# Output projection as side jobs of the top-16 attention, and another order of the first loads, in a graph and transformer kernel on one core

## Chip, cores and metric

The kernel runs on one core of a Trainium2 chip. The metric is the device time of one execution in microseconds.

## What is computed

Node features x (1250 x 512, float32) and 41250 edges (src, dst, sorted by dst) go through four residual layers, each on the normalised rows of x:

```
x = x + gnn0(layernorm(x))      # x@wc + mean over edges of (x@wn)[dst] + bias
x = x + ffn0(layernorm(x))      # causal attention, 8 heads, then a gated mixture of 8 experts
x = x + gnn1(layernorm(x))      # x@W_self.T + neighbour mean @ W_neigh.T, layer norm, gamma, beta
x = x + ffn1(layernorm(x))      # below
return x
```

The last layer (`_L1_ffn_ref`) is

```
x   = x + (depthwise conv over 3 rows + pos_b)
q,k,v = split(x @ qkv_w.T + qkv_b); 8 heads of 64
logits = (q * 512**-0.5) @ k.T                  # 1250 x 1250 a head
_, idx = top_k(logits, 16)                      # per row
attn   = softmax over those 16; out = attn @ v[idx]
return out @ wo_w.T + wo_b
```

## The kernel before

The rows are kept as 10 tiles of 128 (the last of 98) in the SBUF tensor `X` (`NT` = 10, `D` = 512, `KD` = 4 blocks of 128 columns, `H` = 8 heads, `HP` = 4 pairs of heads). The program is a series of stages, each a block in which the five engines run their own instruction lists and meet by semaphores; between stages all engines meet. The change touches the first stage and the last.

**First stage, `graph_in` (L94).** It builds the adjacency counts as a matrix. SP fetches the edges (`raw`, 8 DMAs, L173 and L175), then `wc`, five vectors and `v_b` broadcast to all partitions (L177 to L182), and then the list `ahead` (L185: `wn`, the three attention weights of the next layer, some vectors), all on one queue, one after the other and without waiting. ACT, on its own queue, fetches the node rows X as soon as their padding is zeroed (L396 and L398).

VectorE waits for all edge DMAs (`s_edges`), splits the indices (L234 to L237), reduces the distance of every edge from its window to a flag that says whether a slower general path is needed (`worst`, L241 to L244), and makes three keys (L246 to L249), the third for the general path alone. TensorE transposes `worst` (L333) and then the three keys, 9 transposes (L338); VectorE makes the flag (L252 to L256) and copies the keys to `ends` (L258). Then each engine loads the flag in a register and branches. With these inputs both take the Else side: for each of 323 groups of 128 edges VectorE writes two one-hot tiles (`one_hot`, L264 and L265) into one of `HOTS` = 8 buffers and TensorE multiplies them into a chunk of PSUM (L379), after opening each chunk with a matmul of zeros (L376). ACT copies finished chunks to `AT` (L465), and TensorE turns them (`flip`, L299). Between these, at written group numbers, ACT computes row means (`mean`, L403, for group 10), variances (L411, groups 22 and 36), and the normalised rows, of which TensorE makes the first layer's own projection.

**Last stage, `top_layer` (L1142).** After convolution and the first pair's projections, a loop of `TN` = 80 steps runs, one for each head and tile: n = 20*i + 10*half + t. In step n:
- SP fetched the pair's keys and queries for `half` earlier (L1236), POOL splits them in parts (`stage`).
- TensorE makes scores(n+1) in three banks of PSUM; two steps alternate between banks 0 to 2 and 3 to 5.
- VectorE (`largest`, L1682 to L1690) takes the 8 largest twice and replaces them.
- ACT takes exponentials (L1580, L1586), POOL subtracts (L1284), which leaves the 16 largest; TensorE transposes the result of step n-2 in three pieces through bank 6 (`turn`, L1405), ACT copies each piece (`keep`, L1607, L1602); for each pair of steps TensorE weighs V (`weigh`, L1420) in bank 7, ACT drains it (L1616), and POOL multiplies it by the inverse sums into `QO` (`normalise`, L1293).

Each engine's list of a step is written by hand. Bank 7 also serves side jobs, all on odd steps, in the dictionary `work_at`: the q, k and v projections of the next pair of heads (`qk` jobs of 4 float32 matmuls at steps 1 to 9 after the start of a pair, `v` jobs at 11, 13 and 15), and for the last pair, which has none to prepare, four `wo` jobs at steps 61, 63, 65 and 67 that transpose the output weights. A program counts the evictions before each step (`kept_after`, `jobs_before`, `qkv_jobs`), and these counts are the waits:

```
for b in range(KD):
    work_at[61 + 2 * b] = ("wo", b, None)
...
if (i, half) == (3, 0):
    sp.wait_ge(s_job, qkv_jobs)
    sp.dma_start(raw_wo[:, :, :], rows_of(io["L1_ffn_wo_w"])).then_inc(s_wo_in, 16)
```

TensorE issues a job's parts between the pieces of `turn` (`job`, L1448), ACT evicts it one step later (`keep_job`, L1552). `raw_wo` lies where `ct` (the convolved rows) was, `wo` where the weights `wt` were.

The output projection (`project`, L1462) of tile t is four matmuls over `QO`'s four blocks, one block a pair of heads. Tiles 0 and 1 are issued at the end of step 79, 2 and 3 after step 80, 4 and 5 after 81, and 6 to 9 after 82. POOL has added the output bias to X in steps 0 to 9 (L1313). VectorE adds each projected tile to X (L1706), and SP stores it (L1247).

Of the kernel before, what the change touches and what calls it, by code (L numbers as in the profile page):

```python
# [20 lines left out]
P = 128  # L21
# [72 lines left out]
def graph_in(nc, m, io, space, wc, own, hi, lo, ahead):  # L94
# [39 lines left out]
    with ExitStack() as ctx:  # L134
# [31 lines left out]
        @block.sync  # L166
        def _(sp):
            sp.wait_ge(s_blank, 2)
            for n, name in enumerate(("src", "dst")):
                e = io[name]  # L170
                for g in range(EG):
                    rows = min(P, full - g * P)
                    sp.dma_start(raw[0:rows, n, g, :], e[g * P * P:(g * P + rows) * P].rearrange(  # L173
                        "(t p) -> t p", p=P)).then_inc(s_edges, 16)
                sp.dma_start(raw[last_p:last_p + 1, n, last_g, 0:rest], e[full * P:NE].rearrange(  # L175
                    "(a p) -> a p", a=1)).then_inc(s_edges, 16)
            sp.dma_start(wc[:, :, :], rows_of(io["L0_gnn_wc"])).then_inc(s_wc, 16)  # L177
            for vec, small in ((m.bias0, "L0_gnn_bias"), (m.bias1, "L1_gnn_bias"), (m.gamma1, "L1_gnn_gamma"),
                               (m.beta1, "L1_gnn_beta"), (m.wo_b, "L1_ffn_wo_b")):
                sp.dma_start(vec[:, :], io[small].rearrange("(a d) -> a d", a=1).broadcast_to([P, D])  # L180
                             ).then_inc(s_small, 16)
            sp.dma_start(m.v_b[:, :], io["L1_ffn_qkv_b"][2 * D:3 * D].rearrange("(a d) -> a d", a=1)  # L182
                         .broadcast_to([P, D])).then_inc(s_small, 16)
            for dst, src in ahead[1]:
                sp.dma_start(dst, src).then_inc(ahead[0], 16)  # L185
            sp.wait_ge(s_small, 96)
            sp.wait_ge(ahead[0], 16 * len(ahead[1]))
# [27 lines left out]
        def _(dve):  # L215
# [22 lines left out]
                              ALU.subtract).then_inc(s_split, 1)  # L238
            dve.wait_ge(s_split, 3)
            drel = key[:, 3, :, :].rearrange("p g e -> p (g e)")  # L240
            dve.tensor_reduce(worst[:, 0:1], drel, AX_X, ALU.max).then_inc(s_flag, 1)  # L241
# [3 lines left out]
                                     op0=ALU.add, op1=ALU.max).then_inc(s_flag, 1)  # L245
            dve.tensor_copy(key[:, 0, :, :], part[:, 0, :, :]).then_inc(s_split, 1)  # L246
            dve.scalar_tensor_tensor(out=key[:, 1, :, :], in0=key[:, 3, :, :], scalar=float(NT), in1=part[:, 1, :, :],
                                     op0=ALU.mult, op1=ALU.add).then_inc(s_split, 1)
            dve.scalar_tensor_tensor(out=key[:, 2, :, :], in0=raw[:, 1, :, :], scalar=float(NT), in1=part[:, 1, :, :],  # L249
                                     op0=ALU.mult, op1=ALU.add).then_inc(s_split, 1)  # L250
            dve.wait_ge(s_lined, 1)
# [5 lines left out]
            dve.wait_ge(s_keyed, 1)  # L257
            dve.tensor_copy(ends[:, :, :].rearrange("p n e -> p (n e)"), ps_f[:, 0:3 * EG * P]).then_inc(s_cols, 1)  # L258
            dve.wait_ge(s_cols, 1)
# [12 lines left out]
            scattered = dve.value_load(flag_i[0:1, 0:1], min_val=0, max_val=1)  # L272
            with dve.If(scattered):
                for chunks in (range(0, 3), range(3, NC)):
                    if chunks[0]:
# [18 lines left out]
        def _(pe):  # L294
# [36 lines left out]
            pe.wait_ge(s_made, 3)  # L331
            pe.wait_ge(s_flag, 3)
            pe.transpose(ps_w[:, 0:P], worst[:, 2:3], m.identf[:, :]).then_inc(s_lined, 1)  # L333
            pe.wait_ge(s_split, 6)
            for n in range(3):
                for g in range(EG):
                    c = (n * EG + g) * P
                    mm = pe.transpose(ps_f[:, c:c + P], key[:, n, g, :], m.identf[:, :])  # L338
            mm.then_inc(s_keyed, 1)
            pe.wait_ge(s_cols, 1)  # L340
            pe.wait_ge(s_blank, 3)
# [4 lines left out]
            scattered = pe.value_load(flag_i[0:1, 0:1], min_val=0, max_val=1)  # L346
            with pe.If(scattered):
                for c in range(NC):
                    bank = ps_c[:, c % CHUNKS, :]
# [42 lines left out]
        def _(act):  # L392
            x = io["x"]
            act.wait_ge(s_zeroed, 1)
            for a in (0, 3, 6):
                act.dma_start(m.X[:, a:a + 3, :], x[a * P:(a + 3) * P, :].rearrange("(t p) d -> p t d", p=P)  # L396
                              ).then_inc(s_nodes, 16)
# [744 lines left out]
def top_layer(nc, m, io, space, raw_qk, raw_v, taps, qb, s_ahead, ahead_done, out):  # L1142
# [12 lines left out]
    for i in range(1, HP):  # L1155
        for v, job in enumerate(qk_jobs):
            work_at[2 * NT * (i - 1) + 1 + 2 * v] = ("qk", i, job)
        for v, ts in enumerate(v_groups):
            work_at[2 * NT * (i - 1) + 11 + 2 * v] = ("v", i, ts)
    for b in range(KD):  # L1160
        work_at[61 + 2 * b] = ("wo", b, None)
    evictions, jobs = len(v_groups), len(v_groups)
# [6 lines left out]
    v_kept = [len(v_groups)] + [kept_after[2 * NT * (i - 1) + 11 + 2 * (len(v_groups) - 1)] for i in range(1, HP)]  # L1169
    qkv_jobs = jobs_before[61]  # L1170

    with ExitStack() as ctx:
        s = Stage(nc, m, ctx, "tl")
        (s_zn, s_w_turned, s_w_kept, s_x_turned, s_x_kept, s_edge, s_tapped, s_mid, s_conv, s_first, s_first_kept,
         s_job, s_job_kept, s_wo_in, s_staged_k,
         s_fetched_0, s_fetched_1, s_staged, s_scored, s_max, s_negm, s_read, s_max2, s_topped, s_exp, s_rest,
         s_sum, s_inv, s_blank, s_probs, s_turned, s_kept, s_weighed, s_drained, s_normed, s_biased,
         s_projected, s_final, s_stored) = s.signals(
            "zn w_turned w_kept x_turned x_kept edge tapped mid conv first first_kept job job_kept wo_in staged_k "
            "fetched_0 fetched_1 staged scored max negm read max2 topped exp rest sum inv blank probs turned kept "  # L1180
# [6 lines left out]
        wt = space("tl_wt", 61440, [P, KD, 3 * D])  # L1187
        raw_wo = space("tl_raw_wo", 40960, [P, KD, D])
        wo = space("tl_wo", 61440, [P, KD, D])
# [36 lines left out]
        def _(sp):  # L1226
            sp.wait_ge(s_first_kept, 6)
            for i in range(HP):
                for half in range(2):
# [4 lines left out]
                    for arrived, rows in ((kl, KT[r, i % 2:i % 2 + 1, :]), (qs, QO[r, i:i + 1, :])):  # L1234
                        for to in range(2):
                            sp.dma_start(arrived[to * DH:(to + 1) * DH, half:half + 1, :].bitcast(F32), rows  # L1236
                                         ).then_inc(s_fetched[half], 16)
                    if (i, half) == (3, 0):
                        sp.wait_ge(s_job, qkv_jobs)
                        sp.dma_start(raw_wo[:, :, :], rows_of(io["L1_ffn_wo_w"])).then_inc(s_wo_in, 16)  # L1240
            for half in range(2):
                sp.wait_ge(s_fetched[half], 64 * HP)
            sp.wait_ge(s_wo_in, 16)
            for t in range(NT):
# [6 lines left out]
        def _(pool):  # L1251
# [50 lines left out]
            for n in range(TN + 4):  # L1302
# [7 lines left out]
                if 0 < hi < 2 * HP and step < 5:  # L1310
                    stage(hi, step)
                if n < NT:
                    pool.tensor_tensor(m.X[:, n, :], m.X[:, n, :], m.wo_b[:, :], ALU.add).then_inc(s_biased, 1)  # L1313
                    pool.wait_ge(s_biased, n + 1)

        @block.tensor
        def _(pe):
# [109 lines left out]
            def job(n, part):  # L1427

                kind, i, what = work_at[n]
                if part == 0:  # L1430
                    if n >= 5:
                        pe.wait_ge(s_drained, 2 * ((n - 3) // 2))
                    pe.wait_ge(s_job_kept, kept_after[n - 1])
                    if kind == "wo":
                        pe.wait_ge(s_wo_in, 16)
                if kind == "qk":
# [6 lines left out]
                elif kind == "v":  # L1443
                    if part >= len(what):
                        return
                    mm = project_v(ps_o[:, (what[part] - what[0]) * P:], i, what[part:part + 1])
                else:
                    mm = pe.transpose(ps_o[:, part * P:(part + 1) * P], raw_wo[:, i, part * P:(part + 1) * P],  # L1448
                                      m.identf[:, :])
                last = len(what) - 1 if kind == "v" else KD - 1  # L1450
                if part == last:
                    mm.then_inc(s_job, 1)

            def project(t):
# [4 lines left out]
                if t >= 6:  # L1459
                    pe.wait_ge(s_final, t - 5)  # L1460
                for k in range(KD):
                    mm = pe.matmul(proj_bank(t), QO[:, k, t * P:(t + 1) * P], wo[:, k, :], start=(k == 0),  # L1462
                                   stop=(k == KD - 1))
# [39 lines left out]
        def _(act):  # L1503
# [34 lines left out]
            def keep_job(n):  # L1538
# [8 lines left out]
                elif kind == "v":  # L1547
                    if i >= 2:
                        act.wait_ge(s_weighed, (i - 1) * NT)
                    keep_v(ps_o, i, what)  # L1550
                else:
                    act.copy(wo[:, :, i * P:(i + 1) * P], ps_o.rearrange("p (k c) -> p k c", k=KD)  # L1552
                             ).then_inc(s_job_kept, 1)
# [84 lines left out]
        def _(dve):  # L1638
# [63 lines left out]
            for t in range(NT):  # L1702
                x_t = m.X[:, t, :]
                dve.wait_ge(s_biased, t + 1)
                dve.wait_ge(s_projected, t + 1)
                dve.tensor_tensor(x_t, x_t, proj_bank(t), ALU.add).then_inc(s_final, 1)  # L1706
# [550 lines left out]
```

## Time and profile before

| | us |
|---|---|
| median of 3 runs (1705.13 to 1709.62) | 1708.88 |
| the profiled execution, its own time | 1702.91 |
| its span, from the first to the last instruction | 1701.0 |
| TensorE busy (matmuls) | 1503.1 (88%) |
| VectorE busy | 1036.5 (61%) |
| ACT busy | 724.0 (43%) |
| POOL busy | 541.7 (32%) |
[...]

A busy share is a mean over stages with different limits, so it says little of one stage; the prediction reads stretches of the span instead. L12 stands for line 12 of the kernel. Instruction rows carry, in brackets, how long the engine stood idle before, and what released it; "issue" is time in which it waited for nothing that the profile shows. SPq and ACTq are the DMA queues' issues by SP and ACT.

### The profile page before, as it was taken

What the parts mean: (1) busy time and instruction counts of PE and PEld (TensorE: products, weight loads), DVE (VectorE), ACT (ScalarE), POOL (GpSimd) and SP (SyncE); (2) the same over time, 40 slices, a digit from 0 to 9 for tenths busy, and PEclk for the clock granted to TensorE, in tenths of its full rate; (3) what the DMA queues carried; (4) which work ended last, traced back from release to release, by engine and by line L of the source; (5) the groups of instructions that cost most, each with busy time, mean ns of one, the idle gap of its engine ahead of it and who ended that gap; (6) DMA issues with size and microseconds to landing.
All of it is one profiled execution on the core that took longest, in us unless ns stands there. A gap on an engine that the chain in (4) does not pass through costs nothing. (4 is left out here: it accounts for less than half of the span.)

```text
span 1701.0 us, 22234 instructions
## 1 busy us (share of the span) xinstructions
PE 1503.1 (88%) x8280; PEld 935.3 (55%) x8280; DVE 1036.5 (61%) x2001; ACT 724.0 (43%) x1396; POOL 541.7 (32%) x399
## 2 busy tenths in 40 slices
PE   4888988997787889999999899778999999998778
PEld 2454444445666655454545554455676776776554
DVE  6988443326777741123123322747999999999981
ACT  4343002324555541101101230154778778778771
POOL 0110500005656410000000051005876676667550
PEclk9999999998999998999999999889999999999999
DMA  6000100017121123000000200002101101110001
GB/s 230 1 1 1 77 1 1 0 27 186 37 63 32 33 101 125 0 0 1 1 0 0 60 16 0 1 5 58 21 12 32 32 1 32 32 45 13 2 0 61
DMA packets 28571, 57.03 MB, mean 34 GB/s; under 512 B 7904, under 2 KB 12644, under 8 KB 28208
## 3 DMA queue, kind: packets, MB, share of 16 engines
q1 hardware_dynamic: 27152, 53.03, 11.3%
q10 hardware_dynamic: 1312, 2.56, 0.4%
q8 instruction: 69, 1.13, 0.3%
q14 instruction: 38, 0.31, 0.1%
HBM read 28.77 MB, written 5.84 MB: 20 GB/s over the span
## 5 line engine op out<-in xcount | busy, mean ns | idle before, releaser
L1284 POOL TENSOR_TENSOR tl_ex<-tl_ex,tl_left 128x1250 f32<-128x1250 f32 x80 | 209.8, 2623 | 36.9 <-ACT tl_left L1586 32.8
L1125 DVE SCALAR_TENSOR_TENSOR X<-ex_ps_x,g,X 128x512 f32<-128x512 f32 x80 | 59.9, 751 | 192.6 <-PE ex_ps_x L1018 192.6
L1405 PE MATMUL tl_banks<-identf,tl_ex 128*128 128x128 f32 x800 | 139.5, 290 | 42.1 <-ACT tl_pt L1607 25.6
L991 PE MATMUL ex_ps_h<-yt,w 128*128 128x512 f32 (+1 forms) x384 | 143.8, 529 | 0.0
L1607 ACT COPY tl_pt<-tl_banks 128x512 f32<-128x512 f32 (+1 forms) x200 | 108.1, 541 | 83.7 <-PE tl_banks L1405 81.2
L1405 PEld LDWEIGHTS tl_banks<-identf,tl_ex 128*128 128x128 f32 x800 | 90.1, 144 | 97.4 <-ACT tl_pt L1607 44.3
L1018 PE MATMUL ex_ps_x<-w,hid 128*128 128x512 f32 (+1 forms) x320 | 143.1, 599 | 0.0
L1071 ACT ACTIVATE hid<-ex_ps_h,b 128x512 f32<-128x512 f32 (+1 forms) x48 | 29.1, 608 | 242.2 <-PE ex_ps_h L991 242.2
L1898 POOL TENSOR_TENSOR lo<-xn,hi 128x512 f16<-128x512 f32 x5 | 5.9, 1187 | 379.5 <-ACT hi L1988 379.5
L1586 ACT ACTIVATE tl_left<-tl_left,tl_negm 128x1250 f32<-128x1250 f32 x80 | 107.4, 1343 | 29.3 <-DVE tl_left L1690 29.0
L1682 DVE MAX8 tl_m<-tl_banks 128x8 f32<-128x1250 f32 x80 | 116.4, 1455 | 5.7 <-PE tl_banks L1382 5.6
L1688 DVE MAX8 tl_m<-tl_left 128x8 f32<-128x1250 f32 x80 | 117.1, 1464 | 2.8
L1686 DVE MATCH_REPLACE8 tl_left<-tl_m,tl_banks 128x1250 f32<-128x1250 f32 x80 | 116.0, 1450 | 0.0
L1690 DVE MATCH_REPLACE8 tl_left<-tl_m,tl_left 128x1250 f32<-128x1250 f32 x80 | 115.6, 1446 | 0.0
L991 PEld LDWEIGHTS ex_ps_h<-yt,w 128*128 128x128 f32 x384 | 74.6, 196 | 65.7 <-issue 65.5
L1580 ACT ACTIVATE tl_ex<-tl_banks,tl_negm 128x1250 f32<-128x1250 f32 x80 | 104.7, 1309 | 2.5 <-DVE tl_left L1686 1.3
L1420 PE MATMUL tl_banks<-tl_pt,tl_V 128*64 128x128 f32 x1600 | 104.8, 278 | 0.0
L1018 PEld LDWEIGHTS ex_ps_x<-w,hid 128*128 128x128 f32 (+1 forms) x320 | 60.3, 189 | 73.9 <-issue 73.9
L265 DVE TENSOR_SCALAR hot_m<-ruler,ends 128x320 f16<-128x320 f16 x323 | 98.5, 305 | 0.2 <-issue 0.2
L264 DVE TENSOR_SCALAR hot_b<-ruler,ends 128x128 f16<-128x128 f16 x323 | 86.3, 267 | 15.3 <-PE gi_ps_c L379 14.2
L1420 PEld LDWEIGHTS tl_banks<-tl_pt,tl_V 128*64 128x64 f32 x1600 | 85.7, 137 | 14.1 <-issue 14.1
L1339 PE MATMUL tl_banks<-tl_ct,tl_wt 128*128 128x512 f32 (+1 forms) x192 | 82.0, 554 | 9.4 <-DVE tl_ct L1657 6.2
(272 smaller groups left out, 2944.4 us busy)
## 6 DMA issues: line engine op xcount, KB each, us to landing
kl<-KT SPq DMA_DIRECT2D x16, 320.0 KB, 4.3
qs<-QO SPq DMA_DIRECT2D x16, 320.0 KB, 5.9
tl_kl<-tl_KT SPq DMA_DIRECT2D x16, 320.0 KB, 4.4
tl_qs<-tl_QO SPq DMA_DIRECT2D x16, 320.0 KB, 5.9
w<-in_L_ffn_W SPq DMA_DIRECT2D x8, 512.0 KB
w<-in_L_ffn_W SPq DMA_DIRECT2D x4, 1024.0 KB, 9.0
at_kept<-AT SPq DMA_DIRECT2D x1, 3200.0 KB, 9.0
AT<-at_kept SPq DMA_DIRECT2D x1, 3200.0 KB, 18.8
```

Of the source, the lines that this page charges most:

```text
L991: mm = pe.matmul(h_bank(u)[:, 0:w], w1[e][:, k, j * P:(j + 1) * P], yt[:, G % 2, k, 0:w], start=(k == 0), stop=(k == KD - 1))
L1018: mm = pe.matmul(x_bank(v)[0:rows(t), :], hid[:, (EX * G + e) % HIDS, j, r * P:r * P + rows(t)], w2[:, 2 * e + j, :], start=(j == 0), stop ...
L1284: pool.tensor_tensor(ex[:, n % EXS, 0:N], ex[:, n % EXS, 0:N], left[:, n % LEFT, :], ALU.subtract).then_inc(s_probs, 1)
L1405: mm = pe.transpose(ps_t[:, b * P:(b + 1) * P], ex[:, n % EXS, a + b * P:a + (b + 1) * P], m.identf[:, :])
L1420: mm = pe.matmul(ps_o[u * DH:(u + 1) * DH, 0:P], V[:, h // 2 % 2, k, h % 2 * DH:(h % 2 + 1) * DH], pt[:, (2 * j + u) % PTS, k * P:(k + 1) ...
L1580: act.activation(ex[:, n % EXS, 0:N], logits(n)[:, 0:N], ACT.Exp, bias=negm[:, n:n + 1]).then_inc(s_exp, 1)
L1586: act.activation(lf, lf, ACT.Exp, bias=negm[:, n:n + 1]).then_inc(s_rest, 1)
L1607: act.copy(pt[:, n % PTS, a:a + w], ps_t[:, 0:w]).then_inc(s_kept, 1)
L1682: dve.max(m8[:, n % TOPS, 0:8], logits(n)[:, 0:N]).then_inc(s_max, 1)
L1686: dve.match_replace(lf, m8[:, n % TOPS, 0:8], logits(n)[:, 0:N], TAKEN).then_inc(s_read, 1)
L1688: dve.max(m8[:, n % TOPS, 8:16], lf).then_inc(s_max2, 1)
L1690: dve.match_replace(lf, m8[:, n % TOPS, 8:16], lf, TAKEN).then_inc(s_topped, 1)
```

## The change

First stage:
- SP waits for all edge DMAs to land before it issues `wc` and everything behind it; ACT waits for the same before it issues the node rows.
- VectorE makes the first two keys before the two reductions and the flag. The third key, its three transposes and its copy are now made inside the general path, on the side of the branch that these inputs do not take. TensorE transposes the two keys (6 transposes) first and `worst` after them.

Last stage:
- The output weights are fetched as four DMAs of 128 rows each, into the tiles of the four vectors `bias0`, `bias1`, `gamma1` and `beta1`, which are no longer needed, behind the rows of the second head.
- The four `wo` jobs go to steps 57, 59, 61 and 63.
- Eight new `out` jobs at steps 65 to 79: for tile t = 0 to 7, three matmuls over the first three pairs of heads; ACT copies the result to a tile `partial` (in the place of `ct`), and POOL adds it to X two steps later, before its bias addition in that step's list.
- `project` of tiles 0 to 7 is one matmul; tiles 8 and 9 keep four. VectorE's final sum waits for POOL's addition too.

```diff
             for n, name in enumerate(("src", "dst")):
...
+            sp.wait_ge(s_edges, 16 * 2 * (EG + 1))
             sp.dma_start(wc[:, :, :], rows_of(io["L0_gnn_wc"])).then_inc(s_wc, 16)
...
             dve.wait_ge(s_split, 3)
+            dve.tensor_copy(key[:, 0, :, :], part[:, 0, :, :]).then_inc(s_split, 1)
+            dve.scalar_tensor_tensor(out=key[:, 1, :, :], in0=key[:, 3, :, :], scalar=float(NT), in1=part[:, 1, :, :],
+                                     op0=ALU.mult, op1=ALU.add).then_inc(s_split, 1)
             drel = key[:, 3, :, :].rearrange("p g e -> p (g e)")
             dve.tensor_reduce(worst[:, 0:1], drel, AX_X, ALU.max).then_inc(s_flag, 1)
...
-            dve.tensor_copy(key[:, 0, :, :], part[:, 0, :, :]).then_inc(s_split, 1)
-            dve.scalar_tensor_tensor(out=key[:, 1, :, :], ...
-            dve.scalar_tensor_tensor(out=key[:, 2, :, :], ...
...
-            dve.tensor_copy(ends[:, :, :].rearrange("p n e -> p (n e)"), ps_f[:, 0:3 * EG * P]).then_inc(s_cols, 1)
+            dve.tensor_copy(ends[:, 0:2, :].rearrange("p n e -> p (n e)"), ps_f[:, 0:2 * EG * P]).then_inc(s_cols, 1)
...
             pe.wait_ge(s_made, 3)
-            pe.wait_ge(s_flag, 3)
-            pe.transpose(ps_w[:, 0:P], worst[:, 2:3], m.identf[:, :]).then_inc(s_lined, 1)
-            pe.wait_ge(s_split, 6)
-            for n in range(3):
+            pe.wait_ge(s_split, 5)
+            for n in range(2):
...
             mm.then_inc(s_keyed, 1)
+            pe.wait_ge(s_flag, 3)
+            pe.transpose(ps_w[:, 0:P], worst[:, 2:3], m.identf[:, :]).then_inc(s_lined, 1)
...
             act.wait_ge(s_zeroed, 1)
+            act.wait_ge(s_edges, 16 * 2 * (EG + 1))
             for a in (0, 3, 6):
...
+    EARLY = 8
     for b in range(KD):
-        work_at[61 + 2 * b] = ("wo", b, None)
+        work_at[57 + 2 * b] = ("wo", b, None)
+    for t in range(EARLY):
+        work_at[65 + 2 * t] = ("out", t, None)
...
-                    if (i, half) == (3, 0):
-                        sp.wait_ge(s_job, qkv_jobs)
-                        sp.dma_start(raw_wo[:, :, :], rows_of(io["L1_ffn_wo_w"])).then_inc(s_wo_in, 16)
+                    if (i, half) == (0, 1):
+                        for b in range(KD):
+                            sp.dma_start(raw_wo[b][:, :], io["L1_ffn_wo_w"][b * P:(b + 1) * P, :]).then_inc(s_wo_in, 16)
...
+                if n - 2 in work_at and work_at[n - 2][0] == "out":
+                    t = work_at[n - 2][1]
+                    pool.wait_ge(s_job_kept, kept_after[n - 2])
+                    pool.tensor_tensor(m.X[:, t, :], m.X[:, t, :], partial[:, t, :], ALU.add).then_inc(s_added, 1)
+                    pool.wait_ge(s_added, t + 1)
...
+                    if kind == "out":
+                        pe.wait_ge(s_normed, (2 * HP - 3) * NT // 2 + i // 2 + 1)
...
+                    if part >= HP - 1:
+                        return
+                    mm = pe.matmul(ps_o, QO[:, part, i * P:(i + 1) * P], wo[:, part, :], start=(part == 0),
+                                   stop=(part == HP - 2))
...
-                for k in range(KD):
-                    mm = pe.matmul(proj_bank(t), QO[:, k, t * P:(t + 1) * P], wo[:, k, :], start=(k == 0),
+                ks = range(HP - 1, KD) if t < EARLY else range(KD)
+                for k in ks:
+                    mm = pe.matmul(proj_bank(t), QO[:, k, t * P:(t + 1) * P], wo[:, k, :], start=(k == ks[0]),
                                    stop=(k == KD - 1))
...
+                elif kind == "out":
+                    act.copy(partial[:, i, :], ps_o).then_inc(s_job_kept, 1)
                 else:
+                    act.wait_ge(s_job, qkv_jobs)
...
                 dve.wait_ge(s_biased, t + 1)
+                if t < EARLY:
+                    dve.wait_ge(s_added, t + 1)
```

## Rows read from the trace of the kernel before

**Rows 1.** Timeline, 0 to 27 us: start, us, engine, line, names, idle before.

```profile
5.04 0.33 SPq L175 DMA_DIRECT2D raw<-in_dst  x1
...
10.99 0.36 DVE L234 TENSOR_SCALAR part<-raw 128x384 int32<-128x384 int32 x1 [7.31 <-DMA raw<-in_dst]
...
12.12 0.55 DVE L241 TENSOR_REDUCE worst<-key 128x1 f32<-128x384 f32 x1
...
13.25 0.35 DVE L246 CAST key<-part 128x384 f32<-128x384 int32 x1
...
13.98 0.55 DVE L249 SCALAR_TENSOR_TENSOR key<-raw,part 128x384 f32<-128x384 int32 x1
...
14.45 0.27 DVE L252 TENSOR_REDUCE flag<-gi_ps_s 1x1 f32<-1x128 f32 x1
...
14.59 2.18 PE L338 MATMUL gi_ps_f<-identf,key 128*128 128x128 f32 x9 [0.74 <-DVE key L249]
...
16.81 1.36 DVE L258 COPY ends<-gi_ps_f 128x1152 f32<-128x1152 f32 x1 [1.74 <-PE gi_ps_f L338]
...
25.30 0.60 PE L376 MATMUL gi_ps_c<-ruler,none 128*128 128x510 f16 x1 [6.91 <-issue]
...
26.20 0.25 DVE L264 TENSOR_SCALAR hot_b<-ruler,ends 128x128 f16<-128x128 f16 x1 [3.49 <-PE gi_ps_c L379]
```

**Rows 2.** DMA queues, 6 to 10 us: packets, MB, share of 16 engines.

```profile
q10 hardware_dynamic: 665, 1.30, 88.6%
```

**Rows 3.** DMA queues, 18.2 to 25.3 us.

```profile
q1 hardware_dynamic: 1371, 2.70, 103.4%
q8 instruction: 1, 0.02, 0.9%
```

**Rows 4.** Timeline, 30 to 42 us, ACT and PE.

```profile
30.68 0.59 ACT L465 CAST AT<-gi_ps_c 128x510 f16<-128x510 f32 x1 [9.41 <-PE gi_ps_c L379]
...
40.47 0.60 ACT L465 CAST AT<-gi_ps_c 128x510 f16<-128x510 f32 x1
...
41.13 0.73 PE L299 MATMUL gi_ps_f<-ident,AT 128*128 128x128 f16 x10
```

**Rows 5.** First VectorE pass of the 80 attention steps, tile tl_m.

```profile
L1682 DVE MAX8 tl_m<-tl_banks x80: 1444/1457/1469, 1163.6 to 1647.5; 128x8 f32<-128x1250 f32 x80
```

**Rows 6.** Windows: stretch, us, busy of PE, PEld, DVE, ACT, POOL, clock.

```profile
1270.00:1376.00 106.00, 101.09 (x777) 75.09 (x771) 104.14 (x116) 84.38 (x156) 70.35 (x53) 0.98 0.12 26
1612.00:1629.00 17.00, 11.36 (x92) 8.21 (x91) 16.69 (x19) 13.79 (x27) 10.15 (x8) 0.99 0.00 0
1629.00:1634.00 5.00, 5.00 (x36) 4.14 (x36) 4.90 (x6) 3.69 (x6) 2.61 (x2) 0.71 0.01 3
```

**Rows 7.** POOL's 128x512 addition, tile wo_b.

```profile
L1313 POOL TENSOR_TENSOR X<-X,wo_b x10: 1267/1278/1289, 1165.5 to 1223.7; 128x512 f32<-128x512 f32 x10
```

**Rows 8.** Timeline, 1650 to 1701 us.

```profile
1651.95 7.13 PE L1462 MATMUL tl_banks<-tl_wo,tl_QO 128*128 128x512 f32 x16
...
1658.92 0.60 PE L1405 MATMUL tl_banks<-identf,tl_ex 128*128 128x128 f32 x4
...
1663.64 7.13 PE L1462 MATMUL tl_banks<-tl_wo,tl_QO 128*128 128x512 f32 x16
...
1670.61 0.60 PE L1405 MATMUL tl_banks<-identf,tl_ex 128*128 128x128 f32 x4
...
1674.16 7.13 PE L1462 MATMUL tl_banks<-tl_wo,tl_QO 128*128 128x512 f32 x16
...
1681.23 2.40 PE L1420 MATMUL tl_banks<-tl_pt,tl_V 128*64 128x128 f32 x40
...
1683.56 14.00 PE L1462 MATMUL tl_banks<-tl_wo,tl_QO 128*128 128x512 f32 x32
...
1684.35 0.72 POOL L1293 TENSOR_TENSOR tl_QO<-tl_ot,tl_spread 64x256 f32<-64x256 f32 x1 [11.10 <-ACT tl_ot L1616]
...
1697.67 0.69 DVE L1706 TENSOR_TENSOR X<-X,tl_banks 128x512 f32<-128x512 f32 x1 [2.75 <-PE tl_banks L1462]
```

More of the change, by code:

```diff
@@ L245, in _ @@
                                      op0=ALU.add, op1=ALU.max).then_inc(s_flag, 1)
-            dve.tensor_copy(key[:, 0, :, :], part[:, 0, :, :]).then_inc(s_split, 1)
[L247 to L250, printed above, removed]
             dve.wait_ge(s_lined, 1)
@@ L273, in _ @@
             with dve.If(scattered):
+                dve.scalar_tensor_tensor(out=key[:, 2, :, :], in0=raw[:, 1, :, :], scalar=float(NT),
+                                         in1=part[:, 1, :, :], op0=ALU.mult, op1=ALU.add).then_inc(s_split, 1)
+                dve.wait_ge(s_keyed, 2)
+                dve.tensor_copy(ends[:, 2, :], ps_f[:, 2 * EG * P:3 * EG * P]).then_inc(s_cols, 1)
+                dve.wait_ge(s_cols, 2)
                 for chunks in (range(0, 3), range(3, NC)):
@@ L347, in _ @@
             with pe.If(scattered):
+                pe.wait_ge(s_split, 6)
+                for g in range(EG):
+                    c = (2 * EG + g) * P
+                    mm = pe.transpose(ps_f[:, c:c + P], key[:, 2, g, :], m.identf[:, :])
+                mm.then_inc(s_keyed, 1)
+                pe.wait_ge(s_cols, 2)
                 for c in range(NC):
@@ L1169, in top_layer @@
     v_kept = [len(v_groups)] + [kept_after[2 * NT * (i - 1) + 11 + 2 * (len(v_groups) - 1)] for i in range(1, HP)]
-    qkv_jobs = jobs_before[61]
+    qkv_jobs = jobs_before[57]
     with ExitStack() as ctx:
@@ L1174, in top_layer @@
         (s_zn, s_w_turned, s_w_kept, s_x_turned, s_x_kept, s_edge, s_tapped, s_mid, s_conv, s_first, s_first_kept,
-         s_job, s_job_kept, s_wo_in, s_staged_k,
+         s_job, s_job_kept, s_wo_in, s_added, s_staged_k,
          s_fetched_0, s_fetched_1, s_staged, s_scored, s_max, s_negm, s_read, s_max2, s_topped, s_exp, s_rest,
@@ L1178, in top_layer @@
          s_projected, s_final, s_stored) = s.signals(
-            "zn w_turned w_kept x_turned x_kept edge tapped mid conv first first_kept job job_kept wo_in staged_k "
+            "zn w_turned w_kept x_turned x_kept edge tapped mid conv first first_kept job job_kept wo_in added staged_k "
             "fetched_0 fetched_1 staged scored max negm read max2 topped exp rest sum inv blank probs turned kept "
@@ L1187, in top_layer @@
         wt = space("tl_wt", 61440, [P, KD, 3 * D])
-        raw_wo = space("tl_raw_wo", 40960, [P, KD, D])
+        raw_wo = (m.bias0, m.bias1, m.gamma1, m.beta1)
+        partial = space("tl_partial", 40960, [P, EARLY, D])
         wo = space("tl_wo", 61440, [P, KD, D])
@@ L1237, in _ @@
                                          ).then_inc(s_fetched[half], 16)
-                    if (i, half) == (3, 0):
-                        sp.wait_ge(s_job, qkv_jobs)
-                        sp.dma_start(raw_wo[:, :, :], rows_of(io["L1_ffn_wo_w"])).then_inc(s_wo_in, 16)
+                    if (i, half) == (0, 1):
+                        for b in range(KD):
+                            sp.dma_start(raw_wo[b][:, :], io["L1_ffn_wo_w"][b * P:(b + 1) * P, :]).then_inc(s_wo_in, 16)
             for half in range(2):
                 sp.wait_ge(s_fetched[half], 64 * HP)
-            sp.wait_ge(s_wo_in, 16)
+            sp.wait_ge(s_wo_in, 16 * KD)
             for t in range(NT):
@@ L1434, in job @@
                     if kind == "wo":
-                        pe.wait_ge(s_wo_in, 16)
+                        pe.wait_ge(s_wo_in, 16 * KD)
+                    if kind == "out":
+                        pe.wait_ge(s_normed, (2 * HP - 3) * NT // 2 + i // 2 + 1)
                 if kind == "qk":
@@ L1446, in job @@
                     mm = project_v(ps_o[:, (what[part] - what[0]) * P:], i, what[part:part + 1])
-                else:
-                    mm = pe.transpose(ps_o[:, part * P:(part + 1) * P], raw_wo[:, i, part * P:(part + 1) * P],
-                                      m.identf[:, :])
-                last = len(what) - 1 if kind == "v" else KD - 1
+                elif kind == "wo":
+                    mm = pe.transpose(ps_o[:, part * P:(part + 1) * P], raw_wo[i][:, part * P:(part + 1) * P],
+                                      m.identf[:, :])
+                else:
+                    if part >= HP - 1:
+                        return
+                    mm = pe.matmul(ps_o, QO[:, part, i * P:(i + 1) * P], wo[:, part, :], start=(part == 0),
+                                   stop=(part == HP - 2))
+                last = len(what) - 1 if kind == "v" else HP - 2 if kind == "out" else KD - 1
                 if part == last:
```

## Prediction

> **What bounds the kernel now.** I read the busy shares by stretch first, then the order of time at both ends of the span, then the DMA queues at its start. The kernel is a series of stages, and the edit touches two of them, the first (to about 170 us) and the last (from 1103 us), so only their limits matter.
>
> In the last stage VectorE sets the pace. Its first pass of the 80 attention steps runs from 1163.6 to 1647.5 [rows 5]: 483.9 us over 79 steps, 6.1 us a step, of which four passes of 1.45 us fill nearly all. In the stretch in which most odd steps carry a projection job of 4 matmuls, TensorE is busy 101.1 of 106 us and VectorE 104.1; where no job runs, TensorE is busy 11.4 of 17 us [rows 6]. From 1651.95 us on the roles change: VectorE is done at 1653.6 and TensorE holds the end with the output projection, in pieces of 7.13, 7.13, 7.13 and 14.00 us [rows 8], 40 matmuls in 35.4 us. (Each float32 matmul of 512 columns stands in the trace as two records: x16 is 8 matmuls.) One matmul is thus 14.00/16 = 0.87 us.
>
> In the first stage both VectorE and TensorE wait on a start-up chain. The last edge DMA is issued at 5.04 and VectorE's first edge operation starts at 10.99; TensorE opens the adjacency matrix at 25.30, after 6.91 us in which it waited for nothing the profile shows; VectorE has filled its 8 buffers by then and waits for it until 26.20 [rows 1]. After that the stage runs at VectorE's rate, so what the first matmul gains, the stage's end gains, unless ACT becomes late.
>
> **The tail.** Tiles 0 to 7 leave 3 of their 4 matmuls to steps 65 to 79. That takes 24 x 0.87 = 21 us out of the tail. Not all of it comes back, because the rest of the tail was hidden under these matmuls. Walking the new order from the rows of before [rows 8]:
> - Step 79 has a job of its own, 2.6 us, before the projections that began at 1651.95. TensorE has short waits for ACT's copies there, but those copies shift too; I count 2.3 us (bounds 0 and 2.6): 1654.25.
> - Tiles 0 and 1, one matmul each: 1.74, to 1656.0.
> - Turning and weighing of step 80: it took 1658.92 to 1663.64, 4.7 us; with one more ACT copy in it 4.9, to 1660.9. Tiles 2 and 3: 1.74, to 1662.6.
> - Turning of step 81: 1670.61 to 1674.16, 3.55, to 1666.2. Tiles 4 and 5: 1.74, to 1668.0.
> - Last weighing 1681.23 to 1683.56, 2.33; tiles 6 and 7 1.74, to 1672.0.
> - Tiles 8 and 9 keep four matmuls each: 7.0, to 1679.0. They need POOL's last normalisation, which ended at 1685.07, 1.5 us after the weighing; tiles 6 and 7 (1.74) just cover it. Without that cover it costs up to 1.5.
> - From TensorE's end (1697.56) to the end of the span it was 3.4 us: 1682.4.
>
> That is 1701.0 - 1682.4 = 18.6 us gained. Bounds: 21 (nothing exposed) and 14 (each of the three groups waits another 1.5 us for copies).
>
> **The loop pays for it where there is room.** Each out job puts 3 x 0.87 = 2.6 us on TensorE in an odd step. Two steps last 12.1 us; without jobs TensorE is busy 2 x 6.03 x 11.36/17 = 8.1 of them [rows 6], with the job 10.7. The jobs of 4 matmuls (3.5 us) in the first row of that group are heavier and sit beside VectorE busy 98%, so I cost the out jobs at nothing; without that room each excess microsecond would count eight times. ACT's copy of each partial equals the copy of the jobs it already serves. POOL's 8 added sums cost 1.28 us each [rows 7]; in an odd step POOL then has 0.2 + 2.8 + 0.7 + 1.3 = 5 of 6 us, and nobody waits for it before VectorE's next maximum. The last of them is due before tile 7's final sum, some 5 us after it can run: nothing. VectorE's added wait on them has behind it only its own final sums and SP's stores.
>
> The transposes of the output weights move from steps 61 to 67 to 57 to 63, just behind the last v job, where VectorE is already 0.6 us late; 4 transposes are some 0.7 us: I take 0.3 lost (0 to 1). The weight's fetch moves from one DMA of 1 MB late in the loop to four on SP behind the second head's rows. Nobody needs them for 50 steps; SP has nothing behind them but the next pair's rows, which wait for a job first: nothing.
>
> **The start.** Three edits, one chain.
> - Edges alone on the DMA engines. From 6 to 10 us, q10 with the node rows took 88.6% of the engines [rows 2], and the edges, issued by 5.37, waited behind it 5.5 us. Alone I give them 2.2 us (the last store takes 2.6 from the end of its sum to the end of the span [rows 8]): VectorE starts at 7.5, 3.5 us earlier. Bounds 2.5 and 4.
> - Keys before flag. Between 12.12 and 13.25 stand the two reductions, and the third key took until 14.53 [rows 1]. Without them the second key is done 1.95 us after the start, not 3.5. Six transposes at 2.18/9 = 0.24 take it to 3.4, the flag's transpose to 3.8, three small flag operations (0.6, an estimate from the 0.27 us row) to 4.4, the copy of two thirds of 1.36 us to 5.4 or 5.5; before it ended at 18.17 - 10.99 = 7.2. Gain 1.7.
> - The wait of 6.91 us at the branch. In it one 16 KB instruction packet comes on q8, while q1 keeps the engines full at 103% [rows 3]; so I read it as a fetch of the code behind the branch, queued behind bulk loads, as the edges were 5.5 us behind q10. After the change the branch comes near 13 us, when the node rows (q10) and the weights (q1) are both in flight, so it may wait behind two queues. Bounds: 1.2 us in all if unqueued (5.7 gained) and twice the queue (5.7 lost); I take 2.2 lost, since one queue is sure and the second half over.
>
> [...]
>
> Sum: 3.5 + 1.7 - 2.2 = 3.0 us. A ceiling comes from ACT. The rows now land near 21 us instead of 14.8, and ACT, which had 9.41 us idle at 30.68 and then none until it drained the third chunk at 40.47, is due there again near 38; TensorE's first flip waited for just that (41.13) [rows 4]. A start earlier by 3 leaves that flip on time; by more than about 6 (3 plus what 8 buffers absorb) it would be late, so 6 is the most.
>
> **Total:** 18.6 + 3.0 - 0.3 = 21.3 us off the profiled execution's own 1702.9 gives 1681.6. That execution lies 0.35% under the median of the three runs, 1708.88, and under all of them; I forecast the median: 1708.9 - 21.3 = 1687.6.
>
> **Rivals.**
> 1. The tail gains, the start does not: the fetch waits behind two queues, 5.7 us longer, and the chain's 5.2 is eaten. For it: the edges' own 5.5 us behind one queue. Against: both bursts share the same engines either way. 18.6 - 0.8: 1691.
> [...]
> 3. Slower than before: TensorE becomes the bound of steps 65 to 79. Its place is the scores of the next step, behind an out job; its price is TensorE's work in two steps less 12.1 us, eight times. It eats all 21 us from an excess of 2.7 us, that is at 14.8 us of work, if the clock fell so that 10.7 stretched by 1.4 throughout; 3.2 us excess gives 1713. Against: the heavier jobs ran at clock 0.98.
> 4. The edit does not move what it says: the output projection was hidden. The chain of time at the end shows it was not, so this gets next to nothing.
>
> **Chances.** Forecast (gain 17 to 26) 0.68; rival 1 0.14; rival 2 0.14; rival 3 0.03; rival 4 0.01. About 0.3%, 5 us, is what a measurement of this kernel can tell from no change. Rivals 1 and 2 are still faster by more, rival 2 not always: faster 0.94, same 0.03, slower 0.03. The range takes the ceiling of the start and of the tail (27 us), with the 4 us by which single runs stray below the median, and rival 2 up: 1678 to 1697.
>
> **What would show it.** Right: VectorE's first edge operation near 7.5 us, the opening matmul near 22, projections of 4 records (1.7 us) between the turning groups, the loop's 484 us unchanged, and some 29 us from VectorE's last pass to the end instead of 47. Wrong: steps of 65 to 79 over 6.1 us, a longer wait before the opening matmul, clock under 0.9 in the tail, or TensorE waiting for ACT or POOL between the short projections.

## The result and the profile after

The median of four runs is 1689.44 us (1687.37 to 1694.62), against 1708.02 us for the kernel before (four runs, 1705.13 to 1709.62). The ratio of the two kernels is 0.9903, with a 95% interval of 0.9887 to 0.992. So the change gains 18.6 us by the medians and 16.6 us by the ratio (13.7 to 19.3), where 21.3 were forecast. The profiled execution was the slowest of the four, 1694.62 us with a span of 1692.5; the mean clock granted to TensorE was 0.961 of full speed in it, and 0.970 in the one before.

First the timeline of the changed kernel at its start: start, us, engine, line, names, and the idle time before with its releaser.

```profile
6.06 0.36 DVE L235 TENSOR_SCALAR part<-raw 128x384 int32<-128x384 int32 x1 [2.38 <-DMA raw<-in_dst]
...
8.16 1.51 PE L340 MATMUL gi_ps_f<-identf,key 128*128 128x128 f32 x6 [8.16 <-DVE key L242]
...
10.49 0.94 DVE L257 COPY ends<-gi_ps_f 128x768 f32<-128x768 f32 x1
...
11.48 0.16 PE L349 MATMUL gi_ps_s<-none 128*1 128x1 f16 x1 [1.59 <-DVE ends L257]
...
18.49 0.61 PE L386 MATMUL gi_ps_c<-ruler,none 128*128 128x510 f16 x1 [6.85 <-issue]
...
24.34 0.63 ACT L414 ACTIVATE hi<-X 128x512 f16<-128x512 f32 x1 [13.95 <-DMA X<-in_x]
...
40.48 0.61 ACT L476 CAST AT<-gi_ps_c 128x510 f16<-128x510 f32 x1
...
41.14 1.25 PE L303 MATMUL gi_ps_f<-ident,AT 128*128 128x128 f16 x10 [6.10 <-ACT AT L476]
```

Against [rows 1, 4]: VectorE starts on the edges at 6.06 instead of 10.99, and the opening matmul comes at 18.49 instead of 25.30, 6.8 us earlier. But the first flip stands at 41.14 in both. TensorE now waits 6.10 us for ACT's copy of the third chunk, which ends at 41.09, because ACT began its row means at 24.34, when the node rows had landed.

Next the timeline of its tail, the same columns.

```profile
1658.19 1.12 PE L1475 MATMUL tl_banks<-tl_wo,tl_QO 128*128 128x512 f32 x2 [1.88 <-ACT tl_ot L1647]
...
1662.34 1.88 PE L1490 MATMUL tl_banks<-tl_wo,tl_QO 128*128 128x512 f32 x4
...
1664.06 0.60 PE L1425 MATMUL tl_banks<-identf,tl_ex 128*128 128x128 f32 x4
...
1665.33 0.66 PE L1425 MATMUL tl_banks<-identf,tl_ex 128*128 128x128 f32 x4 [0.68 <-ACT tl_pt L1638]
...
1668.77 1.98 PE L1490 MATMUL tl_banks<-tl_wo,tl_QO 128*128 128x512 f32 x4
...
1674.15 3.64 PE L1490 MATMUL tl_banks<-tl_wo,tl_QO 128*128 128x512 f32 x4
...
1680.05 8.99 PE L1490 MATMUL tl_banks<-tl_wo,tl_QO 128*128 128x512 f32 x20
...
1689.14 0.69 DVE L1739 TENSOR_TENSOR X<-X,tl_banks 128x512 f32<-128x512 f32 x1 [2.74 <-PE tl_banks L1490]
```

The three pieces of 7.13 us [rows 8] have become 1.88, 1.98 and 3.64 us, and the last of 14.00 has become 8.99. The third is odd: the same four records took 1.98 before. The table by stretches (us, busy of PE, PEld, DVE, ACT and POOL, granted clock, DMA) shows why: in it the granted clock, a share of full speed like all clocks here, is 0.53, after 6.1 us at 1.00 in which TensorE was busy 4.75.

```profile
1668.00:1674.10 6.10, 4.75 (x34) 2.80 (x30) 1.37 (x2) 1.70 (x5) 1.51 (x2) 1.00 0.43 163
1674.10:1677.70 3.60, 3.60 (x6) 1.03 (x4) 0.69 (x1) 0.74 (x2) 0.48 (x1) 0.53 0.02 5
```

VectorE's first pass in the loop, from the view of tile `tl_m`, as in [rows 5]:

```profile
L1713 DVE MAX8 tl_m<-tl_banks x80: 1445/1456/1469, 1171.9 to 1655.7; 128x8 f32<-128x1250 f32 x80
```

It spans 483.8 us (483.9 before), so the loop paid nothing. From these rows each span divides in four. The stage's end is the last one-hot matmul, "middle" is all from there to the first pass of the loop, code that the change does not touch, and "tail" all from the start of the last first pass:

| us | first stage's end | middle | loop | tail | span |
|---|---|---|---|---|---|
| before | 166.0 | 997.6 | 483.9 | 53.5 | 1701.0 |
| after | 166.8 | 1005.1 | 483.8 | 36.8 | 1692.5 |

The tail gained 16.7 us. The middle lost 7.5 in this execution; in all twelve profiles of this document, whose kernels share that code, it was between 997.6 and 1008.5, whether or not a kernel had the change. It goes with the granted clock: from 168 to 228 us that was 1.00 before and 0.94 after, and over the whole middle 0.97 and 0.96, with TensorE busy for 895.5 and 902.6 us; the longest, 1008.5 us in e9 below, had 0.95 and TensorE busy for 906.3. Single profiles are therefore compared below by stretch, and whole times by ratios.

### The profile page after: what moved, and what is told of

Read it like the earlier page. It is cut to its first block and busy times, and to the rows that moved or that the text cites. A ratio compares the mean times of both kernels' runs of the same rounds, so it can differ in the third digit from the quotient of the medians.

```text
span 1692.5 us, 22267 instructions
## 1 busy us (share of the span) xinstructions
PE 1505.7 (89%) x8277; PEld 931.7 (55%) x8277; DVE 1035.5 (61%) x2000; ACT 726.8 (43%) x1404; POOL 551.8 (33%) x407
## 3 DMA queue, kind: packets, MB, share of 16 engines
HBM read 28.77 MB, written 5.84 MB: 20 GB/s over the span
## 5 line engine op out<-in xcount | busy, mean ns | idle before, releaser
L263 DVE TENSOR_SCALAR hot_b<-ruler,ends 128x128 f16<-128x128 f16 x323 | 86.0, 266 | 22.9 <-PE gi_ps_c L389 21.3
```

## The experiments

All ratios are to the kernel before, timed beside it on the same chip. "Theory" is mine after the result: the tail carries nearly all, and the start's gain is lost because the node rows land too late.

### One half of the change at a time

`e1_start_only` has the changed first stage and the old `top_layer`; `e2_tail_only` the reverse.

```diff
 e1: def graph_in(...)    # of after
     def top_layer(...)   # of before
 e2: def graph_in(...)    # of before
     def top_layer(...)   # of after
```

> The first stage of the changed kernel with the last stage of before. Theory (rows land too late): the opening matmul comes near 18.5 us, but ACT gets the node rows near 24.3 and the first flip stays near 41.1, so the stage ends at most 1 us earlier and the time is 0.5 to 1.5 us below before, ratio 0.999 to 1.000. Rival (a chance fall of the clock in the profiled execution hid the gain): the opening chain's 6.8 us arrive in full, ratio near 0.996.

> The last stage of the changed kernel with the first stage of before. Theory: the tail alone is worth 16.5 to 18.6 us, ratio 0.989 to 0.990, as much as the whole change, with 29 to 31 us from the last VectorE pass to the end and 484 us of loop. Rival (the start carries a third of the gain): 12 us, ratio 0.993.

The start alone: ratio 1.0013 (0.9998 to 1.0028), 12 runs. The tail alone: 0.9893 (0.987 to 0.9915), the whole gain. The trace of the start alone repeats the changed kernel's: opening matmul at 19.26, rows to ACT at 24.62, first flip at 41.42 after 6.02 us of waiting for ACT. What looked like three edits that gain 6.8 us is worth nothing measurable. So the rival, the whole 6.8 us hidden by a chance fall of the clock, is out. The clock did fall, in the changed kernel from 1.00 to about 0.5 at 29 us, 6 us before TensorE's wait began at 35.05 and after 5 us in which TensorE was busy 4.20. But it did not set the flip, since ACT had hardly a gap from 24.34 on. The same table by stretches, for the changed kernel:

```profile
24.00:29.00 5.00, 4.20 (x23) 1.48 (x23) 5.00 (x28) 4.66 (x15) 0.00 (x0) 1.00 1.05 387
31.00:41.00 10.00, 3.56 (x20) 2.21 (x20) 6.12 (x33) 9.97 (x25) 0.00 (x0) 0.50 0.32 88
```

ACT is busy for 9.97 of the 10 us from 31 to 41. It is the bound here.

What the start keeps behind the flip is small, and here the clock does count. The second flip comes at 59.19 instead of 60.12, and the changed kernel is still 0.9 us ahead at the flip of 120.48 (121.42 before). By the next it is 0.8 us behind (136.99, 136.24), at a clock of 0.91 from 120 to 158 us where the kernel before had 1.00. Four profiles with this first stage, the changed kernel's, e1's and those of e6 and e7 below, end it at 166.8, 168.6, 165.3 and 165.2 us, against 166.0 and 166.1 with the old one (e2).

### When the node rows land

`e3_rows_first` makes SP's large loads wait for the node rows too; `e4_rows_at_once` takes ACT's wait away, so that the rows go out at 2.2 us as before.

```diff
 e3:          sp.wait_ge(s_edges, 16 * 2 * (EG + 1))
     +        sp.wait_ge(s_nodes, 64)
              sp.dma_start(wc[:, :, :], rows_of(io["L0_gnn_wc"])).then_inc(s_wc, 16)
 e4:          act.wait_ge(s_zeroed, 1)
     -        act.wait_ge(s_edges, 16 * 2 * (EG + 1))
```

> The changed kernel, with SP also waiting for the node rows before it issues wc and all behind it. Theory (the rows land too late because they share the engines with SP's loads): the rows land near 14 us instead of 24.3, the first flip comes near 34.3, and the stage keeps 6 to 6.8 us of the opening chain: 5 to 6 us faster than the changed kernel, ratio to before 0.986. The wait before the opening matmul, now behind one queue, stays 5 to 7 us if one full queue is what it costs, and falls from 6.9 only if the second queue lengthened it. Rival (ACT's own chain or the clock sets the flip): the flip stays within 2 us of 41 and the time is that of the changed kernel, ratio 0.990.

> The changed kernel without ACT's wait: the node rows are issued at 2.2 us as before, SP's other loads stay behind the edges. Theory: the edges land late again (near 9 to 10 us, behind q10), the rows land near 13 to 14.5, the opening matmul comes near 22 to 23 us, and the flip near 38: 2 to 4 us faster than the changed kernel, ratio 0.988. Rival (the edges were slow because of SP's own loads, not the rows): the edges land at 6 us all the same and the time equals that of the kernel in which the rows go first.

With the rows first the ratio is 0.9859 (0.9836 to 0.9881), median 1683.11. Its timeline, the same columns:

```profile
15.71 0.63 ACT L415 ACTIVATE hi<-X 128x512 f16<-128x512 f32 x1 [5.74 <-DMA X<-in_x]
...
17.48 0.61 PE L387 MATMUL gi_ps_c<-ruler,none 128*128 128x510 f16 x1 [5.84 <-issue]
...
33.31 0.73 PE L304 MATMUL gi_ps_f<-ident,AT 128*128 128x128 f16 x10
```

The rows land 8.6 us earlier, the flip moves from 41.14 to 33.31 without a wait, and the stage ends at 158.2, 7.8 us before the kernel before. The theory holds; the loads that matter to ACT had shared the engines with loads whose first reader came much later (`wc` at 54.39 us in the changed kernel, the rest later still).

With the rows at once the edges land at 10.88 again, so it was the rows that held the edges up, not SP's loads. The opening matmul comes at 24.06 and the flip at 39.99, each 1 to 2 us later than expected; the stage ends at 164.7, 2.1 us before the changed kernel's profile but only 0.5 before e7's. The ratio, 0.9903 (0.9882 to 0.9923), is that of the changed kernel, so the 2 to 4 us that I expected over it are not seen. Its tail is 35.1 us, with 1.98 where the changed kernel has 3.64: in this execution the clock did not fall there, it was 1.00.

### The wait before the opening matmul

`e5_fetch_alone` holds both groups of loads until the first chunk is closed, long past the branch.

```diff
+            sp.wait_ge(s_closed, 1)
             sp.dma_start(wc[:, :, :], rows_of(io["L0_gnn_wc"])).then_inc(s_wc, 16)
...
+            act.wait_ge(s_closed, 1)
             for a in (0, 3, 6):
```

> The changed kernel, with both the node rows and SP's loads held until the first chunk is closed, so that nothing bulky is in flight at the branch. Theory (the wait before the opening matmul is a fetch queued behind bulk loads): the wait falls from 6.9 to 1.5 to 2.5 us, the opening matmul comes near 14. Rival (it is a fixed cost of the branch): it stays 6 to 7 us. ACT gets the rows later still, near 27 us or more, so the flip and the end of the stage are later than in the changed kernel by 3 to 8 us in both.

It was run once, in 1699.1 us. The DMA queues from 11 to 15.7 us hold two packets of instructions and nothing else, and the wait is still 4.09 us; the timeline row of the matmul and the queue rows:

```profile
15.68 0.61 PE L386 MATMUL gi_ps_c<-ruler,none 128*128 128x510 f16 x1 [4.09 <-issue]
```

```profile
q8 instruction: 1, 0.02, 1.2%
q14 instruction: 1, 0.01, 0.4%
```

Both sides missed. Bulk loads lengthen the wait, but by 2.8 of 6.9 us, and about 4 are there with empty queues. The queue view, taken in narrow windows, says where the rest goes: it gives the start of the one 16 KB packet on q8, here in e5 from 13.2 to 13.5 us, then in the changed kernel from 15.6 to 15.9 us.

```profile
q8 instruction: 1, 0.02, 19.3%
q8 instruction: 1, 0.02, 21.3%
```

Over all twelve profiles (us):

| in flight during the wait | kernels | wait | before the packet starts | from its start to the opening matmul |
|---|---|---|---|---|
| nothing else | e5 | 4.09 | 1.7 | 2.4 |
| the last of the rows, the first of SP's loads | e10 | 4.60 | 2.0 | 2.7 |
| the rows, engines not full (q10 56.1% in e3) | e3, e8, e9 | 5.83 to 5.95 | 3.2 to 3.3 | 2.7 |
| SP's queue, engines full (q1 102.7% in e2) | before, e2, e4 | 6.91 to 7.60 | 4.3 to 5.1 | 2.5 to 2.6 |
| both queues, engines full (q10 53.7%, q1 50.2% in after) | after, e1, e6, e7 | 6.85 to 7.55 | 4.2 to 5.0 | 2.5 to 2.6 |

The last column hardly moves. (That the packet holds the code behind the branch is my inference from its time; e5, the only kernel with nothing else in flight, has one profile.) What bulk loads lengthen is the time before the packet starts, and a second full queue adds nothing to one that can be seen. (In e4 the rows had landed by then, so only SP's queue was full, at 101.4% of the engines from 16.46 to 24.06 us.)

The flip came at 56.15, 15 us late instead of the 3 to 8 I gave, since the rows reached ACT only at 39.36: ACT's chain from the rows to the flip takes 16.8 us here as in the changed kernel (24.34 to 41.14), so the flip follows the rows one for one. The stage ended at 180.1, 13.3 us late.

`e10_flag_first` takes the order of the keys back, on top of e3's waits.

```diff
-            dve.tensor_copy(key[:, 0, :, :], ...)       # the two keys, ahead of the reductions
...
+            dve.tensor_copy(key[:, 0, :, :], ...)       # three keys, behind them
...
-            for n in range(2):
+            for n in range(3):                          # and the flag's transpose ahead
```

> The kernel with the rows first, with the flag's reductions and transpose ahead of the keys and three keys, as before. Theory: VectorE starts at 6.05 us as with the rows first, and the branch comes 1.7 us later, near 13.3 instead of 11.6; the opening matmul near 19, the first flip near 35, and the time 1.7 us above the kernel with the rows first. Rival (the chain is hidden by the fetch of code, which was under way already): the opening matmul stays near 17.5.

The branch comes at 13.20 instead of about 11.5, 1.7 us later as reckoned. But the wait behind it is 4.60 us instead of 5.84, and the opening matmul is late by 0.5 us (17.96):

```profile
17.96 0.61 PE L378 MATMUL gi_ps_c<-ruler,none 128*128 128x510 f16 x1 [4.60 <-issue]
```

The rows were nearly through by then. So the new order is worth 0.5 us there, nearer to the rival than to the theory; the stage ends at 158.7 against 158.2, and the times cannot be told apart (0.9852, 0.9823 to 0.9882).

`e9_rows_first_no_tail` is e3's first stage with the old `top_layer`.

> The first stage with the edges first, the node rows behind them and SP's other loads behind the rows, and the last stage of before. Theory (the start's worth depends on when the rows land): the stage ends 7 to 8 us earlier than before, ratio 0.995 to 0.996. Rival (later stages give it back, as TensorE's clock falls there more often): ratio above 0.998.

Ratio 0.9954 (0.9935 to 0.9973): the start is worth 8 us once the rows come in time. The rival of a gain given back later is out, though its one profile (span 1704.2) has a middle of 1008.5 us, the longest of all.

### The room beside the loop, and the tail

`e6_jobs_twice` does the three matmuls of each job twice; `e7_four_early` sets `EARLY = 4`.

```diff
 e6: -                    mm = pe.matmul(ps_o, QO[:, part, ...], wo[:, part, :], start=(part == 0), ...)
     +                    for u in (2 * part, 2 * part + 1):
     +                        k = u % 3
     +                        mm = pe.matmul(ps_o, QO[:, k, ...], wo[:, k, :], start=(k == 0), ...)
 e7: -    EARLY = 8
     +    EARLY = 4
```

> The changed kernel with the three matmuls of each of the eight side jobs done twice (the first result overwritten), 5.2 us instead of 2.6 in each odd step from 65 on. Theory (TensorE has 12.1 - 10.7 = 1.4 us of room in two steps): two steps become 12.1 + 1.2 = 13.3 us, the loop 8 to 10 us longer, ratio 0.995. Rival (gaps for ACT's copies cannot be filled, so the room was already used up): 2.6 us each, 20 us longer, ratio 1.002. Rival (there is more room than counted): no change, ratio 0.990.

> The changed kernel with four tiles early instead of eight: tiles 0 to 3 with one matmul in the tail, 4 to 9 with four. Theory (TensorE's matmuls bound the tail one for one): 4 x 3 x 0.87 = 10.4 us longer than the changed kernel, less the 2.3 us that step 79 no longer has a job for and the copies that hide again: 8 to 10.4, ratio 0.995 to 0.996. Rival (copies and POOL already set the tail with eight early): 4 to 6 us longer.

Twice the job: ratio 0.9959 (0.9938 to 0.9981), 1700.34 us. The loop grew from 483.8 to 491.6 us:

```profile
L1715 DVE MAX8 tl_m<-tl_banks x80: 1445/1457/1469, 1166.0 to 1657.6; 128x8 f32<-128x1250 f32 x80
```

That is 7.8 us for the seven jobs ahead of the last first pass (that of step 79 lies behind it), but not evenly: the first of them costs nothing and the second 0.5 us, as TensorE had been ahead, and each later one 1.35 to 1.5 us of the 2.6 added, against 1.2 reckoned. Two steps thus have 1.1 to 1.25 us of room left beside a job, not 1.4. Its tail is 40.0 us, 4.9 over the 35.1 of e4 (neither had the clock's fall): the doubled job of step 79 is 2.6 of them, and that job also starts 2.3 us later behind the last first pass (4.8 against 2.5 us), as TensorE is behind by then.

Four early: 0.9935 (0.9913 to 0.9957), which is 5.5 us over the changed kernel's ratio and too wide to choose between theory and rival. The tail does choose: 44.9 us against 36.8, 8.1 longer. Both tails hold one fall of the clock; here it struck step 79's projections, 3.47 us for four records, after 11 us in which TensorE was busy 7.21:

```profile
1651.00:1655.00 4.00, 4.00 (x10) 1.76 (x9) 1.82 (x3) 2.44 (x4) 1.85 (x3) 0.58 0.00 0
```

10.4 us of matmuls moved into the tail, and step 79 has no job for 2.3: 8.1. TensorE's matmuls bound the tail one for one.

`e8_gaps_filled` stands on e3 and puts tiles 2 to 5 between the turning pieces, where TensorE waited.

```diff
                     turn(back, 0)
...
+                if n >= TN and back < TN:
+                    project(2 * (n - TN) + 2)
...
                     turn(back, 1)
...
+                if n >= TN and back < TN:
+                    project(2 * (n - TN) + 3)
...
-                elif n == TN:
-                    project(2)
-                    project(3)
-                elif n == TN + 1:
-                    project(4)
-                    project(5)
```

> The kernel with the rows first, and with the projections of tiles 2 to 5 put between the turning pieces of steps 80 and 81, where TensorE waits 0.68 us three times for an ACT copy. [...] Rival (ACT's copies set the rhythm, and a matmul of 0.87 in a gap of 0.68 delays each of them): 36 to 37 us, no gain.

Its tail, the same columns as above:

```profile
1652.16 1.02 PE L1491 MATMUL tl_banks<-tl_wo,tl_QO 128*128 128x512 f32 x2
...
1653.49 1.02 PE L1491 MATMUL tl_banks<-tl_wo,tl_QO 128*128 128x512 f32 x2
...
1657.80 1.02 PE L1491 MATMUL tl_banks<-tl_wo,tl_QO 128*128 128x512 f32 x2
...
1659.12 1.02 PE L1491 MATMUL tl_banks<-tl_wo,tl_QO 128*128 128x512 f32 x2
...
1664.16 8.99 PE L1491 MATMUL tl_banks<-tl_wo,tl_QO 128*128 128x512 f32 x20
```

I had expected a tail of 33 to 35.5 us and a ratio of 0.984: 1.5 to 2 us from the three waits of 0.68 us, and up to 1.9 from the piece of 3.64 us, if its two matmuls took 0.87 us each. No projection is slow (the clock was 1.00 from 1645.9 to 1664.1 us), and the tail is 33.2 us: 3.6 less than the changed kernel's, 1.9 less than e4's without the clock's fall. Median 1679.75, ratio 0.9832 (0.9805 to 0.9858), the fastest of all: 9.7 us below the changed kernel's median, taken on another occasion. Its interval overlaps that of e3, so the last step is shown by the tail's rows rather than by the time. (Its first stage, e3's word for word, ended at 161.4, 3.2 us after e3's.) That filled gaps keep the clock up is not shown: this is one profile, and with the gaps the clock stayed up in three of seven (e4, e5 and e6; it fell in the changed kernel, e2, e3 and e10).

## Why the prediction was right, and where it was off

**The tail: right in its walk, one term short.** Counted from VectorE's last first pass (1655.7 against 1647.5), the projections of step 79 begin at 1654.1 on the clock of before (1662.34 less 8.23), where the walk had 1654.25. All its later terms came out too but one: tiles 4 and 5 took 3.64 us, not 1.74. The walk gave a gain of 18.6; 16.7 were measured, and 18.4 in e4, where the clock stayed. The fall is no accident of one profile: it came in four of seven with this tail, always in these four records. Rival 2, a tail slower than walked, had such a fall over the last eight matmuls and ACT's copies waiting as well, for a gain of 9 to 14 us; the fall struck four records, and 16.7 us were gained. That gaps in TensorE's work bring it is not shown: in four profiles the clock was 0.53 after a stretch with 4.75 of 6.1 us busy, yet in e4, e5 and e6 it stayed at 1.00 behind the same stretch, also with 4.75 of 6.1. Why it falls in one execution and not in another stays open.

**The loop: right.** The out jobs cost nothing (483.8 us against 483.9), and e6 finds 1.1 to 1.25 us of room behind that, where 1.4 was reckoned. The 0.3 us for the transposes at steps 57 to 63 did not come. Rival 3 needed 2.7 us of excess work in each pair of steps.

**The start: 3.0 us forecast, about nothing found, by wrong steps that partly cancelled.**
- "VectorE starts at 7.5": it was 6.06. Landing took about 1.2 us after the last issue's end (4.90), not 2.2, and that issue ended 0.5 us earlier than before (5.37).
- "Keys before flag, 1.7": from VectorE's start to the branch 5.42 us, against 7.23: 1.8. Right as a size, though the 3.5 us that it sets beside the second key's 1.95 is the third key's end; e10 shows that the fetch gave most of it back.
- "2.2 lost" at the branch: none, 6.85 against 6.91. The bounds were wrong as well: with nothing else in flight it is 4.1 (e5), not 1.2, which is about what VectorE stood idle at its own branch (1.17 us in the kernel before, ahead of its first one-hot tile at 19.34). I took all of the wait for queueing because the edges had waited 5.5 us behind a queue; 2.8 of it is. That a second full queue lengthens the wait was an estimate, and the runs do not show it: 6.91 to 7.60 us behind one full queue, 6.85 to 7.55 behind two. What they do show is one 16 KB packet on q8, there even in empty queues, which starts 2.4 to 2.7 us before the opening matmul in all twelve profiles.
- "The rows now land near 21": this is the step that failed. They came at 24.34, because in two queues they got about half of the engines, and began 4 us later than before. The ceiling was the right idea with the wrong numbers: ACT's chain behind the rows is rigid at 16.8 us, which puts the flip where it was. What the eight buffers gave back was 0.9 us at the second flip, as the first ran at a clock of 0.50 (1.25 us instead of 0.73), and even that was gone by 137 us. Rival 1 had the outcome, a start that gains nothing, by another mechanism.

**The sum.** 18.6 + 3.0 - 0.3 was forecast; the stretches give 16.7 for the tail, 0 for the loop, and -2.6 to 0.9 for the start, by its stage's end in four profiles. By the medians the change gained 18.6, by the ratio 16.6, with an interval from 13.7 to 19.3 us; that the first equals the walk's 18.6 for the tail is chance. The rest of the difference in the profiled execution is the middle's scatter. The total does not choose between the forecast and rival 1: 1687.6 missed the median by 1.8 us and 1691 by 1.6; rival 2's 1697, the upper end of the range, missed it by 7.6. Only the traces do, and they give each a part: the forecast's walk of the tail, and rival 1's start without a gain. Of the signs named for a wrong forecast two came: the clock under 0.9 in the tail, and waits of 0.68 us for ACT between the short projections, which the walk's lengths already held.

## What to carry to other kernels

Before giving a small urgent load a clear road, follow each load pushed back to its first reader, and ask how rigid the work behind it is: here 6.8 us won on one engine were lost at the first place where it met another engine's chain, 16.8 us behind the rows. Order loads by when they are needed, all of them; one more wait turned a start worth nothing into one worth 8 us. At the end of a kernel, work that only waits for its last factor can be done early in the room that a profile shows, and what is left should be placed in the gaps, not behind them (a tail of 33.2 us against 35.1, both without a fall of the clock).

## What the runs showed that was not expected

- Loading the flag and taking the branch on TensorE costs 4.1 us with no other transfer in flight (4.09 idle before the opening matmul in e5), and 6.9 to 7.6 us with the DMA engines full. From the start of the instruction packet on q8 it is 2.4 to 2.7 us in both cases; the queueing is all before it.
- Two full queues shared the engines nearly evenly from 13 to 20 us in the changed kernel: the rows' q10 took 54.1% and SP's q1 49.7%.

```profile
q10 hardware_dynamic: 698, 1.38, 54.1%
q1 hardware_dynamic: 700, 1.28, 49.7%
```

- Untouched code between the two changed stages took 997.6 to 1008.5 us over twelve profiles, more than half of what the whole change is worth.
